# Mixture of experts on one NeuronCore: bias rows loaded by SyncE in place of GpSimd, result rows of single units one unit later

## The reference

```python
logits = xt @ Wr + br
probs = softmax(logits); top_p, top_idx = top_k(probs, 2)
weights = top_p / top_p.sum(axis=-1, keepdims=True)
xn = (xt - mu) * rsqrt(var + LN_EPS)
xe = xn[None] * ln_g[:, None, :] + ln_b[:, None, :]
h = gelu(einsum('end,edh->enh', xe, W1) + b1[:, None, :])
y = einsum('enh,ehd->end', h, W2) + b2[:, None, :]
out = (weights[:, :, None] * y at top_idx).sum(axis=1)
```

## Time and profile before

| | |
|---|---|
| median of 3 runs | 2281.2 us (2279.86 to 2282.58) |
| the profiled execution | 2286.24 us |
| its span, first to last instruction | 2284.5 us |
| mean granted TensorE clock | 0.953 of full |
| PE busy | 2023.8 us (89%) |
| DVE busy | 1136.1 us (50%) |
| POOL busy | 1051.0 us (46%) |
| ACT busy | 606.6 us (27%) |
| expert stage | from about 1849 us to the end |
| bias gathers, L890 | 35 |
| token gathers, L886, and scatters, L898 | 56 each |

### The profile page before, as it was taken

The page is one execution under the profiler, slowest core; times in us unless marked ns, Lnnn a source line. Parts: engine busy times, 40 slices in busy tenths (PEclk is TensorE's granted clock), DMA queues, the critical chain, the costliest instruction groups (busy, mean ns, idle before and its releaser), DMA issues.

```text
span 2284.5 us, 26178 instructions
## 1 busy us (share of the span) xinstructions
PE 2023.8 (89%) x8235; PEld 1382.6 (61%) x8235; DVE 1136.1 (50%) x2348; ACT 606.6 (27%) x1262; POOL 1051.0 (46%) x1049
## 2 busy tenths in 40 slices
PE   7999999979999999999776688889988679999987
PEld 3456446535555555555344456677777568888886
DVE  4999999324333434334566656545545831111111
ACT  2333323311111111112422231222222542222232
POOL 0000000066666666666566666666665124444343
PEclk9999999989999999999988899999999579999999
DMA  7432324345555655565644444333334374444463
GB/s 274 159 129 100 136 118 173 131 152 184 181 182 175 189 176 183 177 184 175 168 124 121 132 142 127 91 88 90 90 92 75 141 265 121 121 120 121 115 177 74
DMA packets 129381, 329.69 MB, mean 144 GB/s; under 512 B 24928, under 2 KB 57728, under 8 KB 127968
## 3 DMA queue, kind: packets, MB, share of 16 engines
q0 software_dynamic: 54672, 134.89, 23.7%
q1 hardware_dynamic: 71280, 191.33, 22.8%
q10 hardware_dynamic: 3296, 1.80, 0.3%
HBM read 199.22 MB, written 128.71 MB: 144 GB/s over the span
## 4 chain that ended last, share of the span: by engine, by line
PE 73%; DVE 9%; issue 6%; another core or an unknown queue 6%; DMA 3%; ACT 2%; POOL 1%; DVEq 0%; ACTq 0%; POOLq 0%
PE bank L576 26%; PE bank L637 14%; PE bank L1794 8%; PE bank L1805 7%; PE bank L1714 4%; PE bank L1723 4%; PE bank L512 3%; PE bank L1626 1%; DVE arena L662 1%; DMA work<-ffn_tokens,work 1%; DVE arena L363 1%; ACT arena L569 1%; DMA out<-xn,work 1%; PE bank L1652 1%
## 5 line engine op out<-in xcount | busy, mean ns | idle before, releaser
L576 PE MATMUL bank<-arena,work 128*128 128x512 f32 x1600 | 753.4, 604 | 42.4 <-ACT arena L569 23.7
L662 DVE TENSOR_TENSOR arena<-arena,bank 128x257 f32 x880 | 370.4, 421 | 616.5 <-PE bank L637 336.3
L637 PE MATMUL bank<-arena 128*128 128x257 f32 x1760 | 494.1, 394 | 86.8 <-DVE arena L662 50.5
L617 POOL DMA_INDIRECT arena<-table_bwd,arena x440 | 430.4, 978 | 231.9 <-issue 96.4
L617 POOL DMA_INDIRECT arena<-table_fwd,arena x440 | 425.2, 966 | 213.3 <-issue 97.3
L576 PEld LDWEIGHTS bank<-arena,work 128*128 128x128 f32 x1600 | 297.6, 192 | 318.3 <-issue 286.1
L637 PEld LDWEIGHTS bank<-arena 128*128 128x128 f32 x1760 | 331.5, 196 | 237.8 <-issue 198.2
L569 ACT ACTIVATE arena<-bank 128x512 f32<-128x512 f32 x400 | 238.9, 599 | 804.0 <-PE bank L576 577.2
L1794 PE MATMUL bank<-xn,arena 128*128 128x256 f32 (+1 forms) x1120 | 204.1, 341 | 0.0
L1547 ACT ACTIVATE arena<-bank,work 128x256 f32<-128x256 f32 (+1 forms) x280 | 120.9, 432 | 299.3 <-PE bank L1794 271.0
L860 POOL MEMSET arena<- 128x6425 f32 x1 | 5.5, 5454 | 423.4 <-PE bank L532 423.4
(11 more groups left out here) (316 smaller groups left out, 1634.7 us busy)
## 6 DMA issues: line engine op xcount, KB each, us to landing
table_fwd<-arena SPq DMA_DIRECT2D x100, 512.0 KB
table_bwd<-arena SPq DMA_DIRECT2D x100, 512.0 KB
arena<-in_W SPq DMA_DIRECT2D x35, 1024.0 KB
arena<-in_W SPq DMA_DIRECT2D x2, 4096.0 KB, 13.5
arena<-table_fwd,arena POOLq DMA_INDIRECT x440
arena<-table_bwd,arena POOLq DMA_INDIRECT x440
mix_rows<-arena SPq DMA_DIRECT2D x25, 256.0 KB
arena<-mix_rows SPq DMA_DIRECT2D x50, 128.0 KB
```

The source lines that it names most:

```text
L576: last = pe.matmul(ps[4 + s % 2][:, :], xT[t % 2][:, k * P:(k + 1) * P], ar(W_off[d] + k * 4096 + c * 512, 512), start=(k == 0), stop=(k = ...
L617: e.indirect_dma_start(msg[b][:, 0:C], None, table[d], bass.IndirectOffsetOnAxis(ap=idx[d][:, n % TE:n % TE + 1], axis=0)).then_inc(s_ga[b ...
L637: pe.matmul(ps[SEG[n % len(SEG)]][:, 0:W], oh[b], msg[b], start=True, stop=True).then_inc(s_sm, 1)
L662: vec.tensor_tensor(to, to, ps[SEG[n % len(SEG)]][:, 0:W], ALU.add).then_inc(s_ac, 1)
```

## The change

The gather of the `aux` rows goes from POOL. SP instead issues a plain load of the 128 rows of the unit's expert, at the register that it already uses for W1, just ahead of the load of W1 and behind a wait that the results of the unit six before are computed, since the ring `aux` now has AR = 6 places (two more in the memory of a table that is no longer in use then). DVE no longer computes `axi`. The order of POOL's scatters is changed for single units: up to unit 23 they stay behind the gather of the unit three later, in unit 24 there is none, and from unit 25 on POOL issues the scatter of unit u-4 behind the gather of unit u.

```diff
--- before.py
+++ after.py
@@ -802,11 +802,11 @@
         csum = work[:, 1825:1825 + NX]
         s_cs = sem("router_sums")
         PIECES = ((0, 0, 8), (0, 8, NT), (1, 0, 8), (1, 8, NT))
-        spare = [work[:, 2900 + j:2901 + j] for j in range(3)]
+        spare = [work[:, 3000 + j:3001 + j] for j in range(3)]
         gx = work[:, 2100:2100 + TX]
         gxi = work[0:1, 2156:2156 + TX].bitcast(i32)
         wsl = work[:, 2212:2212 + TX]
-        xsl, axi, osl = (work[:, 2268 + j * TX:2268 + (j + 1) * TX].bitcast(i32) for j in range(3))
+        xsl, osl = (work[:, 2268 + j * TX:2268 + (j + 1) * TX].bitcast(i32) for j in range(2))
         gtmp = work[:, 2436:2436 + NX * TX].rearrange("p (g q) -> p g q", q=TX)
         gtmp2 = work[:, 0:NX * TX].rearrange("p (g q) -> p g q", q=TX)
         odd, even, pe_, od_, sq_, ce_ = (work[:, 448 + j * NX:448 + (j + 1) * NX] for j in range(6))
@@ -827,8 +827,8 @@
         s_c5, s_t5, s_d, s_dw = sem("counts"), sem("totals"), sem("difference"), sem("ratio")
         s_o5, s_q5, s_m5, s_sl = (sem(n) for n in ("place_onehots", "tile_onehots", "slot_mm", "slots"))
         xg = [work[:, j * C:(j + 1) * C] for j in range(4)]
-        AR = 4
-        aux = [work[:, 4 * C + j * AUX:4 * C + (j + 1) * AUX] for j in range(AR)]
+        AR = 6
+        aux = [work[:, o:o + AUX] for o in (*(4 * C + j * AUX for j in range(4)), 2436, 2436 + AUX)]
         xT7 = [xn[:, j * 512:(j + 1) * 512] for j in range(2)]
         yb = [xn[:, 1024 + j * C:1024 + (j + 1) * C] for j in range(4)]
         w1b = [ar(j * 2 * HID, 2 * HID) for j in range(4)]
@@ -885,10 +885,6 @@
                             G.wait(s_t7, max(v, PAIRS - 1 if u > PAIRS else 0) + 1)
                         e.indirect_dma_start(xg[t % 4], None, xtok, bass.IndirectOffsetOnAxis(
                             ap=xsl[:, t:t + 1], axis=0)).then_inc(s_g7[t % 4], 16)
-                    if u >= AR:
-                        G.wait(s_o7, first(u - AR + 1))
-                    e.indirect_dma_start(aux[u % AR], None, a["aux"], bass.IndirectOffsetOnAxis(
-                        ap=axi[:, first(u):first(u) + 1], axis=0)).then_inc(s_a7[u % AR], 16)
 
                 def add_rows(t):
                     e.wait_ge(s_o7, t + 1)
@@ -900,10 +896,12 @@
 
                 for u in range(UNITS):
                     unit_gather(u)
-                    if u >= 3:
+                    if 3 <= u < PAIRS + 3:
                         for t in tiles(u - 3):
                             add_rows(t)
-                for t in range(first(UNITS - 3), TX):
+                    if u > PAIRS + 3:
+                        add_rows(first(u - 4))
+                for t in range(first(UNITS - 4), TX):
                     add_rows(t)
                 e.wait_ge(s_sc, 16 * TX)
 
@@ -973,6 +971,7 @@
                 e.wait_ge(s_ac, 2 * TE)
                 e.wait_ge(s_ad, TURNS)
                 w1 = a["W1"].rearrange("(x k p) h -> p x k h", k=2, p=P)
+                rows_x = a["aux"].rearrange("(x p) c -> p x c", p=P)
                 w2 = a["W2"].rearrange("(x p) f -> p x f", p=P)
 
                 def output(x0, x1):
@@ -996,6 +995,10 @@
                         e.wait_ge(s_h7, products(u - 3))
                     elif u >= 2:
                         e.wait_ge(s_t7, u - 1)
+                    if u >= AR:
+                        e.wait_ge(s_o7, first(u - AR + 1))
+                    e.dma_start(aux[u % AR].rearrange("p (x c) -> p x c", x=1), rows_x[:, ds(x, 1), :]).then_inc(
+                        s_a7[u % AR], 16)
                     e.dma_start(w1b[u % 4].rearrange("p (x k h) -> p x k h", x=1, k=2),
                                 w1[:, ds(x, 1), :, :]).then_inc(s_w1x[u % 4], 16)
                 for j in range(4):
@@ -1305,7 +1308,6 @@
                     V.link(vec.tensor_reduce(gx, gtmp.rearrange("p g q -> p q g"), AX.X, ALU.add))
                     V.link(ts(gx, gx, float(NX - 1), ALU.min))
                     vec.tensor_copy(gxi, gx[0:1, :]).then_inc(s_sl, 1)
-                    V.link(ts(axi, gx, float(P), ALU.mult, pid, ALU.add))
 
                 for j, c0, c1 in PIECES:
                     hit_, tok_ = ohq[j][:, c0:c1, 1, :], ohq[j][:, c0:c1, 0, :]
```

## The result

The changed kernel took 2277.3 us (median of 11 runs, 2271.2 to 2281.75) against 2282.58 for the kernel before (11 runs, 2279.57 to 2287.22). The ratio is 0.9974, with a 95% interval from 0.9961 to 0.9986: faster by about 5.3 us. Forecast were 2271.1 us, 10.1 us less than the 2281.2 known then, in a range up to 2276.5. The direction was right, the gain is half of the forecast one (about 3 to 9 us by the interval), and the time lies 0.8 us above the range.

A forecast was written before the change was run, and what follows sets the result against it. TensorE was taken as the bound, never idle in pairs, losing time in singles to waits for gathered tokens. 0.2 + 3.3 + 6.6 + 0 = 10.1 us off 2281.2 gave 2271.1 us, range 2266 to 2276.5.

The forecast's parts named there:

- (a): On the chain to the first gather: DVE no longer computes the axi addresses, gain 0.2 us.
- (d): SP's new wait for results of unit u-6, ahead of the W1 loads: price 0.
- (e): Singles from unit 25: scatters one unit later end all token waits after the first, gain 6.6 us.
- the rival on the slower side: In the singles, the chain of scatters becomes the bound: 14 us slower, 2295 us, chance 0.03.
- (f): First gap, near the first singles: its 2.77 us and 1.6 us of low clock stay; 2.0 us either way, taken as 0.
- (c): 35 bias loads on SP, each ahead of a W1 load, 0.38 us of SP each: neither load late, price 0.
- (g): End of the kernel: unmoved, since the last four scatters have no gather behind them.
- (b): Stage start: without POOL's bias gathers, tiles 2 and 3 move up; layer 1 of unit 0 starts 3.3 us earlier, bounds 1.25 to 3.3.
- The rival that closes the first gap: Near the first singles, the first gap closes as well: 14.5 us gained in all, time 2266.7, chance 0.08.

The follow-up runs named there:

- e9: The changed kernel run once more unaltered, with a second profile; ratio 0.9974 to the kernel before.
- e2: The changed kernel with the scatters back in the old order, so only the bias rows move to SP; ratio 0.9988 to the kernel before.
- e11: The changed kernel plus 35 small plain transfers issued by POOL ahead of the expert stage; executed once, whole stage 490.7 us.
- e5: The changed kernel with each unit's bias load issued behind its W1 load instead of ahead; executed once, whole stage 435.4 us.
- e4: The changed kernel with W1 loads of units 24 to 28 cut to 16 of 1024 columns; executed once, whole stage 434.1 us.
- e3: The changed kernel with the gathers of units 23 and 24 issued right behind that of unit 22; ratio 0.9953 to the kernel before.
- e10: The kernel before run once more unaltered, for a second profile; executed once, whole stage 442.6 us.
- e8: e3 with each unit's bias load counted on the semaphore of its W1 load; ratio 0.9942 to the kernel before.
- e1: The kernel before with only the new scatter order in single units, bias rows still on POOL; ratio 0.9976 to the kernel before.
- e6: The changed kernel with bias loads of units 24 to 28 cut to 16 of 268 columns; executed once, whole stage 436.6 us.

## Why the prediction was wrong, point by point

**Steps that held.** (a) With the instruction gone, the first gather comes 10.09 us behind the copy of the expert numbers in place of 10.38: 0.29 for 0.2. (d) SP's new wait costs nothing. It shows (SP's waits, L999, below), but in the trace it comes ahead of the wait for layer 1 (which stands at the bias load, L1000), and SP waited for that one behind it each time. At the boundary results were there at 2158.53 and layer 1 was through at 2162.80. (e) The later scatters end all waits of the singles behind the boundary, at once and in every profile (72.47 or 72.48 us), as worked out. Scatters did not queue up, so the rival on the slower side did not come. The pairs stayed at 14.25 us.

```profile
SPq L1000 <- PE bank L1796: 172.5, 31, 9.5
SPq L999 <- DVE xn L192: 146.0, 29, 6.1
```

**The step that failed is (f)**, together with the price 0 in (c). I had the sign open (2.0 us either way) and took 0, since the bytes stay the same. What the runs show: the boundary took 3.4 us more in the first pair of profiles and 1.5 in the second. On SP, a bias load ahead of the W1 load makes that load 0.52 us later, while the gather of unit 24, which hangs on the scatters, moves by only 0.2 to 0.5. The distance between them shrinks from 2.5 to 2.6 us down to 2.0 to 2.2 (e9, e2, e11), and the time from the gather to its use grows from 3.4 to 3.5 up to 4.2 to 5.3. With W1 issued first (e5) most of the loss went, with a small W1 (e4) the gather landed in 3.85 us, and with the gathers early (e3) the boundary had no wait at all.

The first profile had one thing more. There the gather of unit 23 was used 1.3 us too late (transposes 12.01 us behind unit 22's instead of 10.70). That made layer 1 and with it the next W1 load late, 1.86 us in all against 0.28 for the gather, the distance fell to 1.01 and the time to use rose to 6.57. In e9, e2 and e11 unit 23 was 0.2 to 0.6 us late, and in e4 and e5 not at all. The change opened the way to it, but how much of it comes in one execution is chance.

In (c) I asked only whether SP's own loads would still be in time. They were. I did not ask what they would collide with when they come half a microsecond later.

**(g) failed by 1.6 us.** "The end is unmoved" holds for the scatters to 0.3 us, but POOL's last drain takes 1.27 us more. No row of before gave a reason to expect that, and none explains it now.

**(b) was right, its 3.3 us between the two measured values.** The start gained 3.10 us in the first pair (21.06 to 17.96) and 3.89 in the second, where (a) and (b) said 3.5; less the 0.29 of (a), the gathers' own part is 2.81 and 3.60 us. Tile 3 did take tile 2's place and was there before PE asked for it. The next thing late, which I had not priced, was the first tile of all, and the norm of unit 0 behind it: 4.72 and 4.60 us from the first gather's issue to the transposes, 3.59 and 3.72 before. I put that down to the first loads on SP's queue, now with two bias loads among them. In e11, where that gather went out some 55 us behind them, it is 2.88. What share of the delay is the bias loads' no run shows. One reading of the prediction needs care: it put tile 3's lateness down to a W1 load issued between two gathers. In e10 that load went out at 1682.91, 0.09 us behind tile 3's gather and not ahead of it, and the gather took 5.81 us all the same. The rule of the Trainium skill ("Trainium Kernel Development and Optimization", section Key Constraints), by which only issue time is saved, gives 1.25 us here; the traces have 2.81 and 3.60. Read the other way it holds: moving the bias rows to another queue took nothing off the 16 DMA engines (329.69 MB in both profiles), and part of the gain was paid back by waits for transfers that met them.

**(e)'s size came from one execution.** The 6.6 us was right for its profile; the second profile of the kernel before had 3.6 us there. With the terms of the second pair, 3.9 + 3.6 - 1.5 - 1.7 = 4.3 us, near the 4.2 us between the medians of that chip. With those of the first, 3.1 + 6.5 - 3.4 - 1.6 = 4.6, beside 5.3. So in the first pair (f) and (g) make nearly the whole shortfall, and in the second its largest part is (e), at 3.0 us.

The rival that closes the first gap (14.5 us) needed an edit. With it (e3, e8) the gain is 0.5 to 0.6% of the time.

## What to carry to other kernels

When a load moves to another queue, its own deadline is only half of the question: the loads behind it on that queue start later too, and where a short transfer was just clear of a long one, half a microsecond can put them together. Price that from the distance between the two issues in the trace. And where an engine waits for buffers that are free long before, put the gathers ahead of the scatters in its queue: that one reorder (e3) took 4 to 7 us off the stage, about as much as the whole change it was added to.

## What the runs showed that was not expected

- POOL's last drain was 5.044 us to the nanosecond in four profiles with bias gathers on POOL, 6.310 in nine without, and 6.277 with 35 plain transfers added. The number of semaphores doesn't explain it, nor that of all transfers; the number of indirect ones was not tried.
- The same rows make more packets on SP's queue. In the DMA table of the profile, queue q0 (POOL) went from 54672 to 52992 packets and q1 (SP) from 71280 to 76320, for the same 4.8 MB: 48 packets for a gather, 144 for a load. After the change the table reads:

```profile
q1 hardware_dynamic: 76320, 196.14, 23.9%
q0 software_dynamic: 52992, 130.09, 22.6%
```

- TensorE's clock was not decided by the length of the idle time alone. Behind idle times of 2.77 us (before), 2.70 (e1) and 2.68 us (e10) the granted clock was 0.69 (2175 to 2180), 0.79 (2187 to 2195) and 0.82 (2003 to 2012), so for a part of these stretches at the lower level, 1.2 GHz, and the unit took 8.7 to 8.9 us. Behind 3.19 us (e5) and 3.32 us (e6) it was 1.00, which is 2.4 GHz, and the unit took 7.27. Behind 3.42 us (e11) and 3.84 us (e9) it had fallen again, to 0.70 (2051 to 2060) and 0.79 (2000 to 2008). No run shows what decides.
- One kernel had medians of 2282, 2298 and 2111 us on different chips or at different times, but the stretches of the stage agreed to a microsecond where they had no waits for transfers.
